# Moving the middle block's roots and normalisation from GpSimd to ScalarE, with new slots for the steps around them and a new order at the end of the program

## What is computed

```
x = x + 0.5 * ffn(layernorm(x))        # FFN 1
x = x + mamba(layernorm(x))            # middle block; it adds its own input layernorm(x) back
x = x + 0.5 * ffn(layernorm(x))        # FFN 2, same weights

ffn:   e = argmax(x @ Wg + bg)                      # one of 8 experts per token
       out = gelu(x @ W1[e] + b1[e]) @ W2[e] + b2[e]
mamba: xn = x * rsqrt(mean(x^2) + 1e-6) * norm_w
       xp, z = split(xn @ in_proj.T)                # 2 x 256 channels
       xp = silu(causal_conv4(xp))
       dt, B, C = x_proj(xp);  dt = softplus(dt_proj(dt) + b)
       h_t = exp(dt * A) * h_{t-1} + dt * xp * B    # 256 channels x 16 states, along 256 steps
       out = ((C . h + D * xp) * silu(z)) @ out_proj.T + residual
```

## Time and profile before

| what | value |
|---|---|
| median of 3 runs | 1206.09 us (1205.07 to 1206.83) |
| the profiled execution, its own time | 1204.35 us |
| its span in the profile | 1202.6 us |
| mean granted TensorE clock | 0.943 of full speed |
| busy: PE, DVE, ACT, POOL | 1034.6, 990.0, 917.3, 1052.5 us |

### The profile page before, as it was taken

The page is one execution under the profiler, slowest core; times in us unless marked ns, Lnnn a source line. Parts: engine busy times, 40 slices in busy tenths (PEclk is TensorE's granted clock), DMA queues, the critical chain, the costliest instruction groups (busy, mean ns, idle before and its releaser), DMA issues.

```text
span 1202.6 us, 16666 instructions
## 1 busy us (share of the span) xinstructions
PE 1034.6 (86%) x5380; PEld 546.6 (45%) x5380; DVE 990.0 (82%) x1616; ACT 917.3 (76%) x1403; POOL 1052.5 (88%) x670
## 2 busy tenths in 40 slices
PE   6896869798989999998989899898989986967778
PEld 3452425254545454554545455454545444433246
DVE  2327988999989999999989999999999898988920
ACT  2457676889989888889889888888898796774631
POOL 1139999999999999999999999999999999999810
PEclk9896969899999999999999999999999997969789
DMA  4033433315143434334151433342240524242000
GB/s 104 1 128 130 141 114 133 124 54 189 35 158 107 141 115 143 105 122 145 52 185 57 149 115 134 105 160 106 97 168 21 179 78 149 101 154 97 1 9 18
DMA packets 61750, 130.04 MB, mean 108 GB/s; under 512 B 7552, under 2 KB 28720, under 8 KB 53472
## 3 DMA queue, kind: packets, MB, share of 16 engines
q1 hardware_dynamic: 61664, 128.98, 31.4%
HBM read 106.94 MB, written 22.02 MB: 107 GB/s over the span
## 4 chain that ended last, share of the span: by engine, by line
POOL 57%; issue 16%; PE 14%; ACT 7%; DVE 5%; DMA 1%; SPq 0%; POOLq 0%; DVEq 0%; ACTq 0%
POOL hb L1198 31%; POOL hb L1206 17%; PE PY L636 5%; POOL dt L1222 2%; POOL dtx L1227 2%; PE PH L603 2%; PE dA L616 2%; DVE dA L1021 2%; ACT hs L833 2%; DVE hb L1019 1%; POOL roots L1175 1%; ACT dA L857 1%; POOL xr L1186 1%; PE Y L648 1%; ACT hs L811 1%
## 5 line engine op out<-in xcount | busy, mean ns | idle before, releaser
L1198 POOL TENSOR_TENSOR hb<-dtx_rep,bs 128x1024 f32<-128x1024 f32 x256 | 597.7, 2357 | 1.8 <-DMA dtx_rep<-dtx_rows 1.8
L857 ACT ACTIVATE dA<-dt_rep,A 128x512 f32<-128x512 f32 x512 | 340.7, 689 | 68.2 <-DVE hb L1025 54.4
L1021 DVE TENSOR_TENSOR_SCAN dA<-dA,hb 128x512 f32<-128x512 f32 x256 | 312.3, 1220 | 9.8 <-DVE oh L1063 3.2
L1019 DVE TENSOR_TENSOR_SCAN hb<-dA,hb 128x512 f32<-128x512 f32 x256 | 297.1, 1205 | 26.0 <-ACT dA L857 25.9
L1206 POOL TENSOR_TENSOR hb<-hb,cs 128x1024 f32<-128x1024 f32 x128 | 300.6, 2359 | 5.1 <-DVE hb L1019 5.1
L636 PEld LDWEIGHTS PY<-W,hs 128*128 128x128 f32 x2048 | 250.8, 194 | 76.2 <-issue 73.2
L636 PE MATMUL PY<-W,hs 128*128 128x128 f32 x2048 | 265.7, 281 | 0.0
L603 PE MATMUL PH<-xnT,W 128*128 128x512 f32 x396 | 224.7, 650 | 0.0
L648 PE MATMUL Y<-hb,Sel 128*32 128x512 f32 x1024 | 149.8, 654 | 62.5 <-POOL hb L1206 58.4
L811 ACT COPY hs<-PH 128x512 f32<-128x512 f32 x198 | 115.1, 581 | 115.5 <-PE PH L603 103.3
L1025 DVE TENSOR_TENSOR hb<-dA,cs 128x512 f32<-128x512 f32 x256 | 177.0, 691 | 17.8
(11 more groups left out here) (103 smaller groups left out, 1148.7 us busy)
## 6 DMA issues: line engine op xcount, KB each, us to landing
dtx_rep<-dtx_rows SPq DMA_DIRECT2D x32, 1024.0 KB, 6.3
dt_rep<-dt_rows SPq DMA_DIRECT2D x32, 1024.0 KB, 8.1
bs<-bc_rows SPq DMA_DIRECT2D x64, 256.0 KB, 3.8
cs<-bc_rows SPq DMA_DIRECT2D x64, 256.0 KB, 3.8
dtx_rows<-dtx SPq DMA_DIRECT2D x32, 256.0 KB, 2.5
dt_rows<-dt SPq DMA_DIRECT2D x32, 256.0 KB, 2.7
X<-in_x SPq DMA_DIRECT2D x16, 256.0 KB, 3.1
out<-X SPq DMA_DIRECT2D x16, 256.0 KB, 2.4
```

The lines of the kernel that those rows point to most:

```text
L857: nc.scalar.activation(dA[u % NA][:, :], dt_rep[:, h, g, :], ACT.Exp, scale=A[:, h, g, q:q + 1]).then_inc(decay, 1)
L1019: nc.vector.tensor_tensor_scan(x_in_hb, a, x_in_hb, 0.0, ALU.mult, ALU.add).then_inc(scan, 1)
L1021: nc.vector.tensor_tensor_scan(a, a, x_in_hb, 0.0, ALU.mult, ALU.add).then_inc(scan, 1)
L1198: nc.gpsimd.tensor_tensor(hb[:, s % HR], dtx_rep[:, h, 2 * m:2 * m + 2, :], bs[:, q, None, :].broadcast_to([P, 2, CH]), ALU.mult).then_inc ...
```

## The change

Four things, all in the issue order and in who does what; the arithmetic result is the same up to the way a root is formed.

1. **Roots of the middle block.** For chunks whose step falls in a steady turn (turns 0 to 13) GpSimd no longer forms the two variances and the power. ScalarE does it as two ln (with different scale and bias) and one exp over both, at slot 10.5 just ahead of FFN 2's gelu block (`log_and_roots_p`). GpSimd keeps the negated mean, and makes a shift and the two residual factors.
2. **Normalisation of the middle block.** In the same turns the four tiles of `xr` come from ScalarE (`normalize_p`, slot 11.5, behind the gelu block) instead of from GpSimd.
3. **New slots.** FFN 1's second products stand in slots 5 to 8 (before, 5 to 9); `stats_p` ahead of slot 10's scans; `ln_p`, `x1`, `x0`, `taps` half a slot to a slot later; FFN 1's normalisation behind `taps`; `tap01` between the two units of slot 15 instead of ahead of both.
4. **The end.** In turn 16 the gelus of chunk 14 are made in two parts, the first four experts as soon as their copies are in; VectorE instead of ScalarE normalises chunk 15 and copies its transpose; the second products of chunk 14 are spread between the transposes, the gate and the mask.

The set `POOL_C` of eight slots whose C product is GpSimd's is the same in both kernels; there the change only wraps the test in a function.

```diff
 STEADY = Plan(
...
-            ("dt0", 5, 1), ("oh_f1", 5, 1), ("ln_f2", 9, 0), ("gate_f2", 10, 1), ("oh_f2", 12, 0), ("ln_p", 13, 0),
-            ("x1", 14, 0), ("x0", 14, 1)],
+            ("dt0", 5, 1), ("oh_f1", 5, 1), ("ln_f2", 9, 0), ("gate_f2", 10, 1), ("oh_f2", 12, 0), ("ln_p", 13, 1),
+            ("x1", 14, 1), ("x0", 14, 2)],
...
-    w2=[*[(0, e, s, 1, 2) for e, s in experts(5, 6, 7, 7, 8, 8, 9, 9)],
+    w2=[*[(0, e, s, 1, 2) for e, s in experts(5, 6, 6, 7, 7, 8, 8, 8)],
...
-    act={"silu": 3.0, "bc": 4.0, "dt1": 5.0, "dt0": 5.5, "soft": 6.0, "norm_f2": 7.5, "root_f2": 4.5, "root_f1": 12.5, "res_p": 13.5, "norm_f1": 13.5, "gelu_f2": 10.5, "ln_f2": 9.5, "ln_p": 13.0,
-         "taps": 14.0, "gelu_f1": 15.5},
+    act={"silu": 3.0, "bc": 4.0, "dt1": 5.0, "dt0": 5.5, "soft": 6.0, "norm_f2": 7.5, "root_f2": 4.5,
+         "ln_f2": 9.5, "root_p": 10.5, "gelu_f2": 10.5, "norm_p": 11.5, "ln_p": 13.5,
+         "root_f1": 13.0, "res_p": 13.5, "taps": 14.5, "norm_f1": 15.0, "gelu_f1": 15.5},
...
-         "y_f1": 10.0, "stats_p": 10.5, "gate_f2": 11.0, "stats_f1": 12.0, "oh_f2": 12.0, "tap01": 15.0, "tap2": 15.5},
-    pool={"root_f2": 6.5, "dt": 7.0, "dtx": 7.5, "root_p": 11.0, "norm_p": 11.0, "root_f1": 12.5},
+         "y_f1": 9.5, "stats_p": 10.0, "gate_f2": 11.0, "stats_f1": 12.0, "oh_f2": 12.0, "tap01": 15.25, "tap2": 15.5},
+    pool={"root_f2": 6.5, "dt": 7.0, "dtx": 7.5, "root_p": 11.0, "root_f1": 13.5},
...
 DRAIN = Plan(
...
-    w2=[*[(1, e, 0, 0, -3) for e in range(4, E)], *[(1, e, 4 + e // 4, 1, -2) for e in range(E)],
+    w2=[*[(1, e, 0, 0, -3) for e in range(4, E)], *[(1, e, 3 + e // 2, 1, -2) for e in range(E)],
...
-    act={"gelu_f2": 3.5, "norm_f2": 4.0, "ln_f2": 4.5},
-    dve={"gated1": 0.5, "y_f2": [(1, -3), (6, -2), (15.5, -1)], "out": 1.5, "stats_f2": 2, "gate_f2": 5, "oh_f2": 6.5},
+    act={"gelu_f2_0": 0.5, "gelu_f2_1": 3.5},
+    dve={"gated1": 0.5, "y_f2": [(1, -3), (7, -2), (15.5, -1)], "out": 1.5, "stats_f2": 2, "norm_f2": 4, "ln_f2": 4.5,
+         "gate_f2": 5, "oh_f2": 6.5},
...
+            def log_and_roots_p(it, off):
+                k = 2 * act_roots(2, it.i0 + off)
+                it.wait(act, moments[2], off, 1, 1)
+                it.wait(act, normed[2], off, 1, 0)
+                nc.scalar.activation(var[:, 0, :], mv[:, 2, :, 1], ACT.Ln, bias=eps[:, 0:1])
+                nc.scalar.activation(var[:, 1, :], mv[:, 2, :, 1], ACT.Ln, bias=eps_p[:, 0:1], scale=1.0 + RMS_EPS) \
+                    .then_inc(log_root[2], 1)
+                act.wait_ge(log_root[2], k + 1)
+                nc.scalar.activation(roots[:, :, :], var[:, :, :], ACT.Exp, scale=-0.5).then_inc(log_root[2], 1)
+
+            def normalize_p(it, off):
+                it.wait(act, rooted[2], off, 1, 1)
+                Iteration(it.i0 + off - 1 - OFF["ln_p"]).wait_read(act, g_free, "ln_p")
+                for j in range(J):
+                    last = nc.scalar.activation(xr[:, j, :], rows(it, off, j), ACT.Identity,
+                                                scale=roots[:, 1, j:j + 1], bias=shift[:, 2, j:j + 1])
+                last.then_inc(xr_ready, 1)
...
+            def normalize_last(it):
+                it.wait(dve, rooted[1], -1, 1, 1)
+                it.before().wait_read(dve, g_free, "ln_f2")
+                for j in range(J):
+                    last = nc.vector.tensor_scalar(xn[:, 1, j, :], X[:, it.tiles(-1, j, 1), :], rstd[:, 1, j:j + 1],
+                                                   shift[:, 1, j:j + 1], ALU.mult, ALU.add)
+                last.then_inc(normed[1], 1)
```

62 lines of the change are left out of this document (46 added, 16 removed).

## The result

The changed kernel takes 1231.59 us (median of four runs, 1228.02 to 1236.81); the kernel before, run beside it, 1206.42. The ratio is 1.0207 (95% interval 1.0177 to 1.0236): 25.2 us slower, where 11.5 were forecast. The direction and most places were right, the size was not. Two executions of the experiments further down, one of 1218.80 us of e8 and one of 3270.95 of e11, count as slow and are not in their ratios.

The account below looks back on a forecast made before the run. The prediction took a loop through ScalarE, TensorE and VectorE, not GpSimd, to bound full turns. Full turns +28, thin turns -7.5 and end -9 gave +11.5 us: 1217.5 us, own range 1205 to 1231, overall range 1188 to 1232.

Parts of the forecast that it names:

- What bounds the kernel: Full turns: a loop without GpSimd bounds; GpSimd's relief alone is worth half a microsecond, additions to the loop count in full.
- The loop of 65.9 us without GpSimd: Full turn, through ScalarE, TensorE and VectorE: 66.43 us, of which 65.9 are left without GpSimd's 0.49 us.
- the 0.49 us: TensorE's wait for GpSimd before the state sum in a full turn, taken out by GpSimd's relief.
- From the copy to the gelu block: Full turns, ScalarE's copy out of PH to FFN 2's gelu block: plus 1.2 us (0.7 to 1.7).
- From u24 to u1: Full turns, u24 to the next turn's u1, normalisation now in between: plus 1.3 us (0.4 to 2.0).
- the 9.6 taken: Time from u24 until x1 and the next first product are done on TensorE: 9.6 us.
- the full turns: Turns 2 to 12: each grows by 2.5 us (1.8 to 3.2), eleven by 28 us (20 to 35).
- The clock: Rival: longer full turns, with TensorE's waits around x1, bring its clock to 0.9; 1242 us, chance 0.06.
- The thin turns: Turns 0, 1 and 13, where GpSimd bounds: minus 2.5 us each, minus 7.5 us together (3 to 10.5).
- The end: After the last roots: TensorE's 7.29 us idling and 0.78 us mask wait filled; minus 9 us (7 to 10).
- GpSimd as the only bound: Rival: GpSimd bounds after all, a turn shortens by 1.8 us; 1172 us, chance 0.06.
- ScalarE does absorb 1.54 us in its idle time: Rival: ScalarE takes the new work in idle time, full turns stay as they are; 1189.6 us, chance 0.19.

Follow-up runs that it names:

- e8: Kernel before with GpSimd relieved: multiplication for the power, 16 of 128 columns normalised, nothing moved to ScalarE; 1206.14 us, ratio 0.9985.
- e11: Changed kernel with the first skip term (1.02 us of TensorE) moved from slot 8 to slot 4; 1223.03 us, ratio 1.0131.
- e6: Kernel before with four idle ScalarE operations of the normalisation's shape behind u25 (11.5); 1221.80 us, ratio 1.0125.
- e5: Kernel before with only the changed slots of FFN 1's second products, y_f1 and the middle statistics; 1225.37 us, ratio 1.0144.
- e17: Changed kernel with two filling TensorE products a turn and FFN 2's second product of expert 2 earlier in slot 15; 1218.73 us, ratio 1.0089.
- e4: Changed kernel with the middle block's normalisation back on GpSimd, roots still on ScalarE; 1218.87 us, ratio 1.0095.
- e3: Changed kernel with two more TensorE products a turn in two of its waits, result overwritten unread; 1224.19 us, ratio 1.0155.
- e2: Changed kernel with the last FFN as it was before; 1241.35 us, ratio 1.0291.
- e7: Kernel before with four idle ScalarE operations of the normalisation's shape ahead of slot 9 (8.5); 1205.33 us, ratio 0.9987.
- e13: Kernel before with changed last FFN, FFN 2's second products one place earlier, skip term in slot 4, GpSimd relieved by leaving work out; 1175.84 us, ratio 0.9747.

## Why the prediction was right or wrong

**What bounds the kernel: half right.** The loop of 65.9 us without GpSimd is there (e8: 65.87), and at full clock relief of GpSimd alone shortens a turn by 0.7 us, where half a microsecond was said. What is added to ScalarE's loop counts almost in full only when counted from there: e6's 1.54 us made 67.31, 1.44 more than 65.87 but 0.74 more than the kernel before, where GpSimd holds the turn longer. In the sum this was allowed for, since the 0.49 us were taken out first.

**From the copy to the gelu block: right**, 1.21 us for 1.2 (1.06 against the mean of two neighbouring turns before), about half of it the new slots (e5) and half the roots.

**From u24 to u1: right mechanism, too small**, 1.86 us for 1.3, inside its bounds. Up to the scaled residual the step held. Then `x1` and the first product came 0.27 us later than the 9.6 taken, and FFN 1's normalisation, behind the taps, delayed the copy of slot 15 and through it expert 2's second product, for which the copy ahead of u1 waited (0.31 us, e17). The normalisation itself was 1.0 us and not 1.54 (e4); the rest is order. At full clock the full turns cost 31.8 us (e3's turns 2 to 12, 763.3 us, against 731.4) where 28 were forecast.

**The clock: the step that failed.** It was a rival of 0.06, with the waits around `x1` as its cause; it belonged into the sum. The new order makes TensorE wait 1.56 and up to 1.84 us at FFN 2's gelu block, ahead of `x1` and not around it; in ten of eleven full turns its clock then falls to 1.2 GHz, and costs time in those where this meets the loop: 7.4 us by e3. The prediction saw that TensorE would wait in this order, priced the wait and put the slower clock at nothing in its sum. The Trainium skill (Perfetto Trace Analysis, Matmul Optimizations) says that "the matmul engine dynamically scales power based on utilization"; the trace agrees as far as e3's filled waits kept 1.00 and gave 7.4 us; that equal waits of 2.05 us came with a fall and without one (e8), this sentence does not tell.

**The thin turns: the other step that failed.** Turns 0 and 13 gained 5.4 us for the 5.0 forecast, in part by luck: turn 13 took 63.68 us, but 66.47 in e2, whose turns are the same and where the two gained 2.4. Turn 1 gained nothing in any kernel with the changed order (67.5 to 70.5 us against 66.98). The row read for it is half a microsecond short of the turn (66.50 for 66.98), so GpSimd idled 1.6 us in it and not 1.1. It showed TensorE at 0.95 already; with the changed order turn 1 has 0.88 to 0.95. That the added waits lower its clock is not shown: in the old order it took 70.45 us at 0.90 in e7 and, with GpSimd relieved, 72.29 at 0.88 in e8, but 65.67 at 0.97 in e13. So minus 2.5 became plus 0.5 to plus 3.6.

**The end: right**, 10 us for 9.

In sum: +31.8 for the full turns at full clock, +7.4 for their clock, -10 for the end, -5.4 for turns 0 and 13 and +0.5 to +3.6 for turn 1 make 24 to 27, from medians and single profiles together; measured 25.2. Of the 13.7 that the forecast lacked, the clock is 7.4, turn 1 some 3 to 6, the full turns 3.8, and the end takes 1 back.

**The rivals.** GpSimd as the only bound is refuted by e8: at full clock, so without the loss that its 0.9985 contains, a turn is 0.7 us shorter, not 1.8 to 2.4, and GpSimd idles 2.3 of 65.87 us. The Trainium skill (Perfetto Trace Analysis, Identifying the Most-Contended Engine) would have had GpSimd, 98% busy in a turn, optimised first; here relief alone shortened a turn at full clock by 0.7 us and gained no time (e8), and e13 shows that with the second loop shortened as well it pays. ScalarE does absorb 1.54 us in its idle time, but ahead of the copy of slot 9 (e7), not where the change put it (e6): the place decides, as the prediction argued.

**Still open.** Why the clock in one turn falls ahead of work that matters and in the next ahead of work that doesn't, with the same waits, why waits of 2.05 us come with a fall in one turn of e8 and without one in the next, and why turn 1 stays below 1.00 in e3, was not settled. FFN 1's normalisation back ahead of the taps was not tried.

## What to carry to other kernels

Price a new wait of TensorE twice: by its length, and by the slower clock that may follow it; a cheap test is a product without use in the wait. When an engine is 98% busy and its relief gives nothing, look at single turns with their granted clock first, then for a second loop of nearly the same length, and shorten both before judging either. Moved work is paid by its place: the same 1.5 us were free ahead of one wait and cost 15 us over the kernel behind it, half of that by the clock.

## What the chip showed that was not expected

The same wait of TensorE is followed by a fall of its clock in one turn and not in the next. The wait ahead of slot 15 is 2.05 us in turn 3 of the kernel before and in five turns of e7, all at 1.00. In e8 it is 2.05 or 2.06 us in turns 5 to 11: 5, 7, 9 and 11 keep 1.00 and take 65.9 us, 6, 8 and 10 have 0.97 and take 67.3 to 67.6. Where the fall comes behind this wait it costs about 1.4 us in each of three kernels (67.30 against 65.87 in e8, 68.42 against 66.99 in e5, 68.70 against 67.31 in e6). A kernel with some 30 us more TensorE work was 7.4 us faster (e3). And a fall of the clock for 6 us may cost nothing (turn 7 of the changed kernel, 69.51 us) or 1.5 us (turn 5), by what it meets.
